# Attention stage of a decoder layer: sums through a three-bank ring, compact inverses, five transfers per chain, values of two blocks a visit

## The chip, the cores and the metric

One NeuronCore of a Trainium2 chip runs the whole program. The metric is the device time of one execution in microseconds (us). TensorE is written PE, VectorE DVE, ScalarE ACT, GpSimd POOL and the queue that issues most transfers SP.

## The reference

The program is one decoder layer on x of shape (2, 2048, 512): attention with 16 heads of 32, then a cross attention to 77 context rows, then a quantised feed-forward part. The change is in the attention alone, which computes for every batch and head

```
short = softmax(q ks^T / sqrt(32) - |i - j| (1 - decay)) vs
long  = softmax(q kl^T / sqrt(32)) vl
out   = sigmoid(mix) * short + (1 - sigmoid(mix)) * long
```

with 2048 queries and 2048 keys. All other stages are the same in both kernels.

## The kernel before

The attention works in units of one head and one kind of attention: w = 0 and 2 are "short", w = 1 and 3 "long", of two heads; four units make a pass, 16 passes make 64 units. The first and the last pass are written out, the others stand in a loop.

A unit has 16 key blocks of 128 keys (kb, also called a step i) and four query chunks of 512 (qt), so 64 chunks. For each unit five things happen, on different engines:

- **Maxima.** PE makes scores with queries on the partitions (`scores_for_max`, tile `scores_qk`, four PSUM banks used as two pairs). DVE reduces each pair of banks, 128x1024, to a row maximum (`max_pair`, L868). `negate` (L872), `turn_max` (L882) and SP's `place_max` (L735, four small transfers for a long unit, eight for a short one) put the negated maxima as one more row into the query operand.
- **Scores for exp.** PE makes the scores again with keys on the partitions (`scores_for_exp`, tile `scores_kq`, two PSUM banks), the maximum already subtracted. ACT takes exp of each 128x512 chunk into one of eight block buffers (`probs`, L852). Short units add small "kink" matmuls on the diagonal, in both kinds of scores.
- **Values.** `times_v` (L1025): four f32 matmuls, in four column groups of 32, shown as eight records, add a block's product to the bank `po`.
- **Sums.** The 16 blocks of a unit are added up elementwise, before PE's ones-matmuls (`count`, L1032) add over the partitions into the bank `pc`. POOL adds ten blocks (nine `tensor_tensor` of 128x2048, L804). Six blocks (0, 3, 6, 9, 12, 15) are summed by a chain of transfers of 1 MB that POOL issues: the first copies (L813), the others accumulate (L816), each after the one before has landed.
- **End of a unit.** DVE copies `po` out (`take`, L895, at i = 15), inverts `pc` in four pieces of 128x128 (`invert`, L900, at i = 7 to 10 of the next unit), multiplies (`weigh`, L910, i = 11) and, for the second unit of a head, adds the two (`mix`, i = 12). SP stores the result (L742) and loads the operands of the next pass.

PE's order is written by hand: in step i first the values of block i, then eight score chunks in the order exp, max, exp, max, max, exp, max, exp. ACT may write a block buffer only when the values, and the add or the landing of the transfer, of the block eight before are done. Every engine works through its list in order, and so does each queue.

Of the kernel before, what the change touches and what calls it, by code (L numbers as in the profile page):

```python
# [593 lines left out]

TURN_MAX = 10
SQUARE = 32
INVERT = 7
WEIGH = 11
MIX = 12


BY_DMA = (0, 3, 6, 9, 12, 15)
BY_POOL = tuple(b for b in range(KB) if b not in BY_DMA)
ADDS = len(BY_POOL) - 1
POURS = len(BY_DMA)
COUNT_ADDED = KB + 4
COUNT_POURED = KB + 6
POOL_ORDER = (0, 2, 4, 3, 5, 7, 6, 8, 10, 9, 11, 13, 12, 14, 15)
# [16 lines left out]

def attend(nc, qk_scr, v_scr, gates, kinkA, kinkB, pos_scr, attn_scr):

    with ExitStack() as ctx:
# [15 lines left out]

        oT = sb("o_T", [P, 2, BANK], F32)
        o_w = sb("o_weighed", [P, BANK], F32)
# [26 lines left out]
        counted = Rises(sem("a_counted"), UNITS, credit=1)  # L676
        counted_poured = Rises(sem("a_counted_poured"), UNITS, credit=1)
        taken = Rises(sem("a_o_taken"), UNITS, credit=1)
        inverted = Rises(sem("a_inverted"), UNITS * NQ)
# [27 lines left out]
        def _(sp):  # L707
# [21 lines left out]
            def place_max(w, n):  # L729

                sp.wait_ge(turned.sem, turned.at(n, w + 1))
                for dst in (q_op[w], q_up[w]) if w % 2 == 0 else (q_op[w],):
                    row = dst[MROW:MROW + 1, :].rearrange("o (t b c) -> o t b c", t=KB, c=SQUARE)
                    for b in range(P // SQUARE):
                        sp.dma_start(row[:, :, b, :], maxT[b * SQUARE:b * SQUARE + KB, w % 2, :]).then_inc(maxrow[w].sem, 16)  # L735

            def store(p, n):

                sp.wait_ge(mixed.sem, mixed.at(n, p + 1))
# [32 lines left out]
            one_pass(PASSES - 1, False, True)  # L772
            store(1, PASSES - 1)
# [4 lines left out]
        def _(pool):  # L778
            give_credit(pool, [maxed, expd, summed, added, counted, taken, weighed, counted_poured] + stored)
# [14 lines left out]
            def add(w, n, b):  # L794
# [3 lines left out]
                if b == BY_POOL[1]:  # L798
                    first = probs[:, BY_POOL[0], :]
                    wait_apart(pool, counted, counted.at(n, w - 1), passed)  # L800
# [3 lines left out]
                nc.gpsimd.tensor_tensor(total, first, probs[:, b % PBUF, :], ALU.add).then_inc(added.sem, 1)  # L804

            def pour(w, n, b):
# [4 lines left out]
                if i == 0:  # L811
                    wait_apart(pool, counted_poured, counted_poured.at(n, w - 1), passed)
                    nc.gpsimd.dma_start(total, probs[:, b % PBUF, :]).then_inc(landed.sem, 16)  # L813
                else:
                    wait_apart(pool, landed, landed.at(n, w // 2 * POURS + i), passed)
                    nc.gpsimd.dma_start(total, probs[:, b % PBUF, :], accum_op=ALU.add).then_inc(landed.sem, 16)  # L816
# [18 lines left out]
        def _(act):  # L835
            load_positions(act, 0)

            def one_pass(n, first, last):
                for w in range(UNITS):
                    for kb in range(KB):  # L840

                        u, b = divmod(w * KB + kb - PBUF, KB)
                        act.wait_ge(summed.sem, summed.at(n, u * KB + b + 1))
                        if b in BY_POOL:
                            act.wait_ge(added.sem, added.at(n, u * ADDS + adds_until(b)))
                        elif u >= 0 or not first:
                            landed = poured[u % 2]
                            act.wait_ge(landed.sem, landed.at(n, u // 2 * POURS + BY_DMA.index(b) + 1))
                        for qt in range(NQ):
                            k = (w * KB + kb) * NQ + qt  # L850
                            act.wait_ge(scoredB.sem, scoredB.at(n, k + 1))
                            nc.scalar.activation(probs[:, kb % PBUF, qt * BANK:(qt + 1) * BANK], pb[:, k % 2, :], ACT.Exp)\  # L852
                                .then_inc(expd.sem, 1)
# [5 lines left out]
            one_pass(PASSES - 1, False, True)  # L859

        @block.vector
        def _(dve):
# [29 lines left out]
            def take(w, n):  # L892

                dve.wait_ge(summed.sem, summed.at(n, (w + 1) * KB))
                nc.vector.tensor_copy(oT[:, w % 2, :], po[:, :]).then_inc(taken.sem, 1)  # L895

            def invert(w, n, r):

                dve.wait_ge(counted_poured.sem, counted_poured.at(n, w + 1))
                nc.vector.reciprocal(pc[:, r * P:(r + 1) * P], pc[:, r * P:(r + 1) * P]).then_inc(inverted.sem, 1)  # L900

            def weigh(w, n):

                dve.wait_ge(taken.sem, taken.at(n, w + 1))
                dve.wait_ge(inverted.sem, inverted.at(n, (w + 1) * NQ))
                if w == 2:
                    dve.wait_ge(mixed.sem, mixed.at(n, 1))
                elif w == 0 and (not isinstance(n, int) or n > 0):
                    dve.wait_ge(mixed.sem, mixed.before(n, 2))
                nc.vector.scalar_tensor_tensor(pc[:, :] if w % 2 else o_w[:, :], oT[:, w % 2, :],  # L910
# [787 lines left out]
```

## Time and profile before

| | before |
|---|---|
| median of 3 runs | 4902.25 us (4900.92 to 4911.55) |
| profiled execution: time / span | 4901.64 us / 4899.8 us |
| mean granted TensorE clock | 0.98 |
| PE / DVE / ACT / POOL busy over the span | 95% / 80% / 60% / 67% |
| attention, first to last copy of a unit's output | 598.8 to 3780.1 us |

A row of the timeline gives the start and the duration in us, the engine, the line, the operation, the tiles and shapes and, in brackets, how long the engine sat idle before it and for whom. "x4" is four instructions in a row. A PE matmul's duration (0.38 us for 512 columns) is longer than the distance from its start to the next one's (0.22 us), because they overlap.

### The profile page before, as it was taken

How to read it: one execution, taken by the hardware profiler on the slowest of the kernel's cores; microseconds unless marked ns; L12 is line 12 of the kernel's file. 1: busy time of each engine (PE TensorE's matmuls, PEld its weight loads, DVE VectorE, ACT ScalarE, POOL GpSimd, SP SyncE). 2: the span in 40 equal slices, each digit the busy share in tenths (PEclk: the TensorE clock that was granted, in tenths of full speed). 3: DMA queues.
4: the chain of work that ended last, by engine and by line, in shares of the span. 5: the costliest groups of instructions: out<-in, count | busy, mean ns of one | idle time of the engine just before them, and what ended most of it. 6: DMA issues, size and time to landing. Idle time of an engine off the chain costs nothing. (4 is left out here: it accounts for less than half of the span.)

```text
span 4899.8 us, 94453 instructions
## 1 busy us (share of the span) xinstructions
PE 4676.8 (95%) x30732; PEld 2051.3 (42%) x30732; DVE 3911.0 (80%) x4625; ACT 2928.4 (60%) x5106; POOL 3278.3 (67%) x1268
## 2 busy tenths in 40 slices
PE   8998999999999999999999999999998799999998
PEld 3444233333333333333333333333332577777776
DVE  7567888888888888888888888888884588888887
ACT  3222367676766766766666666766666355555554
POOL 0000399998989989888898989989897233333332
PEclk9999799999999999999999999999999799999999
DMA  5444366666676666666666676666765100000000
GB/s 171 126 140 129 84 154 154 152 151 160 146 156 151 157 157 146 159 144 157 153 146 159 144 158 155 157 154 146 165 135 118 59 27 27 20 27 27 27 23 12
DMA packets 216646, 592.18 MB, mean 121 GB/s; under 512 B 46259, under 2 KB 120115, under 8 KB 167157
## 3 DMA queue, kind: packets, MB, share of 16 engines
q0 software_dynamic: 55008, 400.58, 37.6%
q1 hardware_dynamic: 161135, 185.60, 12.8%
q8 instruction: 258, 4.23, 0.3%
q14 instruction: 207, 1.70, 0.1%
q10 hardware_dynamic: 38, 0.08, 0.0%
HBM read 123.56 MB, written 61.64 MB: 38 GB/s over the span
## 5 line engine op out<-in xcount | busy, mean ns | idle before, releaser
L852 ACT ACTIVATE probs_T<-scores_kq 128x512 f32<-128x512 f32 x4096 | 2247.2, 595 | 992.3 <-PE scores_kq L959 819.4
L868 DVE TENSOR_REDUCE rowmax_parts<-scores_qk 128x1 f32<-128x1024 f32 x2048 | 2398.3, 1210 | 546.1 <-PE scores_qk L959 541.9
L804 POOL TENSOR_TENSOR probs_added<-probs_added,probs_T 128x2048 f32<-128x2048 f32 x510 | 2386.1, 4679 | 48.8 <-POOL probs_added L804 37.5
L959 PE MATMUL scores_kq<-q_operand,k_operand 103*128 103x512 f16 (+3 forms) x3712 | 1277.7, 350 | 77.9 <-ACT probs_T L852 69.0
L959 PE MATMUL scores_qk<-k_operand,q_operand 96*128 96x512 f16 (+4 forms) x3712 | 1125.0, 351 | 32.7 <-DVE rowmax_parts L868 17.0
L1025 PE MATMUL outputs_T<-probs_T,v_operand 128*32 128x512 f32 x8192 | 1095.7, 607 | 1.0 <-ACT probs_T L852 1.0
L959 PEld LDWEIGHTS scores_kq<-q_operand,k_operand 103*128 103x128 f16 x3712 | 358.5, 97 | 1072.6 <-ACT probs_T L852 842.0
L959 PEld LDWEIGHTS scores_qk<-k_operand,q_operand 96*128 96x128 f16 (+1 forms) x3712 | 362.4, 98 | 336.8 <-DVE rowmax_parts L868 101.7
L1647 PE MATMUL f_gate_up<-w_gate_up,xq_T 128*128 128x256 f16 (+1 forms) x4608 | 494.3, 266 | 7.7 <-DVE hidden L1538 6.5
L1647 PEld LDWEIGHTS f_gate_up<-w_gate_up,xq_T 128*128 128x128 f16 x4608 | 421.1, 98 | 77.0 <-issue 24.3
L816 POOL DMA_DIRECT2D probs_poured<-probs_T x318 | 275.8, 867 | 255.7 <-DMA probs_poured<-probs_T 186.9
L959 PE MATMUL scores_kq<-q_operand_above,k_operand 103*128 103x512 f16 (+3 forms) x1152 | 400.5, 348 | 1.9 <-ACT probs_T L852 1.5
L959 PE MATMUL scores_qk<-k_operand,q_operand_above 102*128 102x512 f16 (+3 forms) x1152 | 368.8, 351 | 0.0
L1355 POOL TENSOR_TENSOR hidden_parts<-hidden_q,hidden_parts 128x768 f16<-128x768 f32 x64 | 97.9, 1529 | 349.9 <-ACT hidden_parts L1430 349.9
L780 POOL MEMSET ones<- 128x32 f32 x1 | 0.1, 124 | 464.0 <-POOLq L216 464.0
L804 POOL TENSOR_TENSOR probs_added<-probs_T 128x2048 f32<-128x2048 f32 x64 | 296.9, 4639 | 14.6 <-ACT probs_T L852 14.6
L959 PEld LDWEIGHTS scores_kq<-q_operand_above,k_operand 103*128 103x128 f16 x1152 | 110.0, 96 | 434.0 <-ACT probs_T L852 424.8
L1025 PEld LDWEIGHTS outputs_T<-probs_T,v_operand 128*32 128x32 f32 x8192 | 161.8, 108 | 261.8 <-issue 251.7
L900 DVE RECIPROCAL sums<-sums 128x128 f32<-128x128 f32 x256 | 243.8, 954 | 25.7 <-PE sums L1032 25.7
L555 PE MATMUL products_p<-xn_T_parts,w_qkv_parts 128*128 128x512 f16 x1152 | 254.5, 381 | 2.9 <-DVE xn_T_parts L408 1.5
L1632 PE MATMUL f_down<-w_down,hidden_T 128*128 128x512 f16 x1056 | 245.3, 382 | 0.0
L555 PEld LDWEIGHTS products_p<-xn_T_parts,w_qkv_parts 128*128 128x128 f16 x1152 | 112.9, 98 | 136.5 <-issue 4.1
(166 smaller groups left out, 4113.9 us busy)
## 6 DMA issues: line engine op xcount, KB each, us to landing
probs_poured<-probs_T POOLq DMA_DIRECT2D x382, 1024.0 KB, 7.6
qk_parts_dram<-qk_parts SPq DMA_DIRECT2D x96, 256.0 KB, 2.9
q_operand<-qk_parts_dram SPq DMA_DIRECT2D x192, 128.0 KB, 3.4
k_operand<-qk_parts_dram SPq DMA_DIRECT2D x192, 128.0 KB, 4.0
v_dram<-v_heads SPq DMA_DIRECT2D x16, 1024.0 KB, 6.4
v_operand<-v_dram SPq DMA_DIRECT2D x64, 256.0 KB, 6.5
q_operand_above<-qk_parts_dram SPq DMA_DIRECT2D x96, 128.0 KB, 2.8
x_groups<-x SPq DMA_DIRECT2D x8, 1024.0 KB, 9.4
```

Of the source, the lines that this page charges most:

```text
L555: last = nc.tensor.matmul(mm[:, m % 4, :], w_parts[:, a, c, m * P:(m + 1) * P], xT[:, u, c, b, :], start=c == 0 and a == b, stop=c == KT - ...
L780: nc.gpsimd.memset(ones[:, :], 1.0).then_inc(consts, 1)
L804: nc.gpsimd.tensor_tensor(total, first, probs[:, b % PBUF, :], ALU.add).then_inc(added.sem, 1)
L816: nc.gpsimd.dma_start(total, probs[:, b % PBUF, :], accum_op=ALU.add).then_inc(landed.sem, 16)
L852: nc.scalar.activation(probs[:, kb % PBUF, qt * BANK:(qt + 1) * BANK], pb[:, k % 2, :], ACT.Exp)\
L868: nc.vector.reduce_max(rowmax[:, w % 2, g // 2, g % 2:g % 2 + 1], half, AX.X).then_inc(maxed.sem, 1)
L900: nc.vector.reciprocal(pc[:, r * P:(r + 1) * P], pc[:, r * P:(r + 1) * P]).then_inc(inverted.sem, 1)
L959: return nc.tensor.matmul(out, lhsT, rhs, start=start, stop=stop, skip_group_check=True)
L1025: last = nc.tensor.matmul(po[qt * HD:(qt + 1) * HD, :], v_op[:, w, kb, :], probs[:, kb % PBUF, qt * BANK:(qt + 1) * BANK], start=kb == 0, ...
L1355: nc.gpsimd.tensor_tensor(h16[:, 1, a:a + w], hq[:, a:a + w], h16[:, 0, a:a + w], ALU.subtract)\
L1632: last = nc.tensor.matmul(pd[:, :], hT[:, c, a, :], wd[:, c, b, :], start=opens and c == first and a == b, stop=ends and c == first + coun ...
L1647: last = nc.tensor.matmul(pg[:, k % 2, g, 0:w], xqT[:, n % 2, c, a, :], w_up[:, c, g, b, at:at + w], start=c == 0 and a == b, stop=c == KT ...
```

## The change

- **Ring of three banks.** `scores_kq` has three banks. A unit has 66 ring slots: 64 chunks and two slots (`COUNT_SLOTS`, 27 and 36) into which the two ones-matmul groups of the unit before go. The bank `pc` is gone.
- **Values of two blocks a visit.** PE does `times_v` for steps i and i+1 together, then 16 score chunks in the order exp, max, max, exp, four times. Scores for exp run three chunks ahead of the values (`LEAD`).
- **Sums.** ACT writes exp of block 0 straight into `poured_sum`, so the chain has five transfers, all accumulating. POOL adds blocks 1, 2, 4, 5, 7, 8, 10, 11, 13, 14, still nine adds; the order of adds and transfers is changed (`POOL_ORDER`).
- **End of a unit.** ACT copies `po` (`take`) and the two sum banks (`copy_sums`). The sums are packed by two transfers to 128x16 (`pack_sums`), added (`merge`) and inverted (`invert`) by DVE at i = 9, stored to DRAM (`store_inverse`) and spread from there over 128x512 (`spread_inverse`). `weigh` is at i = 13, `mix` at i = 14, both on SBUF tiles. SP's list has the packing and storing ahead of `place_max`, the spreading behind it.

```diff
-INVERT = 7
-WEIGH = 11
-MIX = 12
-BY_DMA = (0, 3, 6, 9, 12, 15)
-POOL_ORDER = (0, 2, 4, 3, 5, 7, 6, 8, 10, 9, 11, 13, 12, 14, 15)
+INVERT = 9
+WEIGH = 13
+MIX = 14
+VISIT = 2
+LEAD = 3
+COUNTS_AT = (4, 6)
+BY_DMA = (3, 6, 9, 12, 15)
+BY_POOL = (1, 2, 4, 5, 7, 8, 10, 11, 13, 14)
+POOL_ORDER = (2, 3, 4, 5, 6, 7, 8, 9, 10, 11, 12, 13, 14, 15)
+def emitted(i):
+    return (i + VISIT) * NQ + LEAD
+COUNT_SLOTS = (emitted(COUNTS_AT[0]), emitted(COUNTS_AT[1]) + 1)
+RING = CHUNKS + 2
+BANKS = 3
...
-        pb = ps("scores_kq", [P, 2, BANK], F32)
+        pb = ps("scores_kq", [P, BANKS, BANK], F32)
-        pc = ps("sums", [P, BANK], F32)
+        def block_of(w, kb):
+            return poured_sum[:, w % 2, :] if kb == 0 else probs[:, kb % PBUF, :]
...
@@ block.sync @@
+            def pack_sums(w, n, j):
+                wait_apart(sp, sums_out, sums_out.at(n, 2 * w + j + 1), passed)
+                wait_apart(sp, merged, merged.at(n, w), passed)
+                sp.dma_start(sums_c[:, j, :], sums[::HD, j, :]).then_inc(packed[j].sem, 16)
+            def store_inverse(w, n):
+                wait_apart(sp, inverted, inverted.at(n, w + 1), passed)
+                wait_apart(sp, inv_spread, inv_spread.at(n, w - 1), passed)
+                sp.dma_start(inv_scr[w % 2:w % 2 + 1, :].rearrange("o (p i) -> (o p) i", i=COMPACT), inv_c[:, :])\
+                    .then_inc(inv_stored.sem, 16)
+            def spread_inverse(w, n):
+                wait_apart(sp, inv_stored, inv_stored.at(n, w + 1), passed)
+                wait_apart(sp, weighed, weighed.at(n, w - 1), passed)
+                rows4 = inv_scr[w % 2].rearrange("(q n) -> q n", q=NQ).unsqueeze(1).to_broadcast([NQ, HD, BANK])
+                sp.dma_start(inv[:, w % 2, :], rows4).then_inc(inv_spread.sem, 16)
...
                 for w in range(UNITS):
+                    back = unit_before(w, n, first)
+                    if back:
+                        for j in range(2):
+                            pack_sums(*back, j)
+                        store_inverse(*back)
                     if after(w, n, last):
                         place_max(*after(w, n, last))
+                    if back:
+                        spread_inverse(*back)
...
@@ block.scalar @@
+            def copy_sums(w, n, j):
+                act.wait_ge(counted[j].sem, counted[j].at(n, w + 1))
+                act.wait_ge(packed[j].sem, packed[j].at(n, w))
+                nc.scalar.copy(sums[:, j, :], pb[:, COUNT_SLOTS[j] % BANKS, :]).then_inc(sums_out.sem, 1)
+            def take(w, n):
+                act.wait_ge(summed.sem, summed.at(n, (w + 1) * KB))
...
+                nc.scalar.copy(oT[:, w % 2, :], po[:, :]).then_inc(taken.sem, 1)
...
@@ block.vector @@
-                nc.vector.reciprocal(pc[:, r * P:(r + 1) * P], pc[:, r * P:(r + 1) * P]).then_inc(inverted.sem, 1)
+            def merge(w, n):
...
+                nc.vector.tensor_tensor(sums_c[:, 0, :], sums_c[:, 0, :], sums_c[:, 1, :], ALU.add).then_inc(merged.sem, 1)
+            def invert(w, n):
+                dve.wait_ge(inv_stored.sem, inv_stored.at(n, w))
+                nc.vector.reciprocal(inv_c[:, :], sums_c[:, 0, :]).then_inc(inverted.sem, 1)
             def weigh(w, n):
                 dve.wait_ge(taken.sem, taken.at(n, w + 1))
+                dve.wait_ge(inv_spread.sem, inv_spread.at(n, w + 1))
...
@@ block.tensor @@
+            def bank_free(w, n, r):
+                r -= BANKS
...
-                        times_v(w, n, i)
-                        counts(w, n, i)
...
+                    for i in range(0, KB, VISIT):
+                        for step in range(i, i + VISIT):
+                            times_v(w, n, step)
+                        if back and i == COUNTS_AT[0]:
+                            count_added(*back)
+                        if back and i == COUNTS_AT[1]:
+                            count_poured(*back)
+                        at = emitted(i)
+                        for step in range(i, i + VISIT):
+                            for half in range(2):
+                                scores(at)
+                                maxima(step, 2 * half)
+                                scores(at + 1)
+                                at += 2
```

## Rows read from the trace of the kernel before

**Rows 1.** Busy time by engine in the attention; columns PE, PEld, DVE, ACT, POOL
```profile
598.83:3780.12 3181.29, 3094.67 (x20017) 1028.41 (x20019) 2613.55 (x2508) 2210.55 (x4030) 2872.35 (x944) 1.00 0.67 152
```

**Rows 2.** The copy of a unit's output: all 64, duration and first and last start
```profile
L895 DVE COPY o_T<-outputs_T x64: 678/680/692, 598.8 to 3780.1; 128x512 f32<-128x512 f32 x64
```

**Rows 3.** Waits from 600 to 3700 us: total, times, longest
```profile
POOL probs_poured L816 <- DMA probs_poured<-probs_T: 183.1, 60, 5.4
ACT probs_T L852 <- DMA probs_poured<-probs_T: 110.8, 77, 3.4
```

**Rows 4.** Timeline of POOL around the end of one unit
```profile
2513.63 0.87 POOL L816 DMA_DIRECT2D probs_poured<-probs_T  x1
...
2523.73 0.87 POOL L816 DMA_DIRECT2D probs_poured<-probs_T  x1
2524.34 4.83 POOL L804 TENSOR_TENSOR probs_added<-probs_added,probs_T 128x2048 f32<-128x2048 f32 x1
2534.18 0.87 POOL L816 DMA_DIRECT2D probs_poured<-probs_T  x1 [5.01 <-DMA probs_poured<-probs_T]
2534.97 0.64 POOL L813 DMA_DIRECT2D probs_poured<-probs_T  x1
```

**Rows 5.** Timeline of ACT, its waits for transfers: the one at the same place
```profile
2533.71 3.37 ACT L852 ACTIVATE probs_T<-scores_kq 128x512 f32<-128x512 f32 x6 [2.57 <-DMA probs_poured<-probs_T]
```

**Rows 6.** Timeline of DVE: the shortest full unit, by the copies of its output
```profile
2111.80 0.68 DVE L895 COPY o_T<-outputs_T 128x512 f32<-128x512 f32 x1
...
2160.56 0.68 DVE L895 COPY o_T<-outputs_T 128x512 f32<-128x512 f32 x1
```

**Rows 7.** Timeline of one undisturbed step, all engines
```profile
2476.45 0.39 PE L959 MATMUL scores_kq<-q_operand,k_operand 103*128 103x512 f16 x1
...
2476.87 2.29 ACT L852 ACTIVATE probs_T<-scores_kq 128x512 f32<-128x512 f32 x4 [0.67 <-PE scores_kq L959]
...
2477.11 0.59 PE L959 MATMUL scores_qk<-k_operand,q_operand 96*128 96x512 f16 x2
...
2477.53 2.35 DVE L868 TENSOR_REDUCE rowmax_parts<-scores_qk 128x1 f32<-128x1024 f32 x2 [0.61 <-PE scores_qk L959]
...
2478.09 0.38 PE L959 MATMUL scores_kq<-q_operand,k_operand 103*128 103x512 f16 x1
...
2478.41 1.06 PE L1025 MATMUL outputs_T<-probs_T,v_operand 128*32 128x512 f32 x8
...
2479.40 0.39 PE L959 MATMUL scores_kq<-q_operand,k_operand 103*128 103x512 f16 x1
```

**Rows 8.** Timeline: values and a count back to back, then the next score
```profile
2485.06 1.07 PE L1025 MATMUL outputs_T<-probs_T,v_operand 128*32 128x512 f32 x8
...
2486.91 0.39 PE L959 MATMUL scores_kq<-q_operand,k_operand 103*128 103x512 f16 x1
```

**Rows 9.** Groups of DVE from 600 to 3700 us: busy us, mean ns
```profile
L900 DVE RECIPROCAL sums<-sums 128x128 f32<-128x128 f32 x244 | 233.2, 956 | 0.0
...
L882 DVE STREAM_TRANSPOSE negmax_T<-negmax 128x32 f16<-128x32 f16 x61 | 11.9, 195 | 0.0
```

**Rows 10.** Timeline of SP: the eight transfers of the maxima of a short unit
```profile
2559.80 2.55 SPq L735 DMA_DIRECT2D q_operand<-negmax_T  x4
2562.39 2.98 SPq L735 DMA_DIRECT2D q_operand_above<-negmax_T  x4
```

**Rows 11.** Transfers of the whole span: KB each, median us from issue to landing
```profile
probs_poured<-probs_T POOLq DMA_DIRECT2D x382, 1024.0 KB, 7.6
...
q_operand<-qk_parts_dram SPq DMA_DIRECT2D x192, 128.0 KB, 3.4
...
v_operand<-v_dram SPq DMA_DIRECT2D x64, 256.0 KB, 6.5
...
attn_T<-attention_dram SPq DMA_DIRECT2D x32, 256.0 KB, 2.8
...
q_operand<-negmax_T SPq DMA_DIRECT2D x256, 1.0 KB, 2.1
```

More of the change, by code:

```diff
@@ L838, in one_pass @@
             def one_pass(n, first, last):
                 for w in range(UNITS):
+                    back = unit_before(w, n, first)
                     for kb in range(KB):
[L842 to L848, printed above, removed]
@@ L849, in one_pass @@
-                        for qt in range(NQ):
[L850 to L853, printed above, removed]
+                        block_free(w, n, kb, first)
+                        for qt in range(NQ):
+                            c = kb * NQ + qt
+                            for j in range(2):
+                                if back and ring_of(c) == COUNT_SLOTS[j] + 1:
+                                    copy_sums(*back, j)
+                            act.wait_ge(scoredB.sem, scoredB.at(n, w * CHUNKS + c + 1))
+                            nc.scalar.activation(block_of(w, kb)[:, qt * BANK:(qt + 1) * BANK], pb[:, ring_of(c) % BANKS, :],
+                                                 ACT.Exp).then_inc(expd.sem, 1)
+                            if back and c == LEAD - 1:
+                                take(*back)
@@ L923, in one_pass @@
                     for i in range(KB):
-                        if i == KB - 1:
-                            take(w, n)
-                        if back and INVERT <= i < INVERT + NQ:
-                            invert(*back, i - INVERT)
+                        distance, chunks = chunks_of(i)
+                        unit = after(w, n, last, distance)
+                        if back and i == INVERT:
+                            merge(*back)
                         if back and i == WEIGH:
                             weigh(*back)
-                        distance, chunks = chunks_of(i)
-                        unit = after(w, n, last, distance)
+                        if back and i == MIX and back[0] % 2:
+                            mix(back[0] // 2, back[1])
                         for c in chunks[::2] if unit else ():
@@ L935, in one_pass @@
                                 negate(*unit)
-                            if i == TURN_MAX and c == chunks[0]:
-                                turn_max(*ahead)
+                            if c == chunks[0]:
+                                if back and i == INVERT:
+                                    dve.wait_ge(merged.sem, merged.at(back[1], back[0] + 1))
+                                    invert(*back)
+                                if i == TURN_MAX:
+                                    turn_max(*ahead)
+                        if back and i == INVERT and not unit:
+                            dve.wait_ge(merged.sem, merged.at(back[1], back[0] + 1))
+                            invert(*back)
                         if i == TURN_MAX and ahead and not unit:
                             turn_max(*ahead)
-                        if back and i == MIX and back[0] % 2:
-                            mix(back[0] // 2, back[1])
             one_pass(0, True, False)
@@ L947, in _ @@
             one_pass(PASSES - 1, False, True)
[L948 to L949 removed]
+            dve.wait_ge(packed[0].sem, packed[0].at(PASSES - 1, UNITS))
+            invert(UNITS - 1, PASSES - 1)
             weigh(UNITS - 1, PASSES - 1)
```

168 lines of the change are left out of this document (87 added, 81 removed).

## The prediction, made before the change was run

> **What bounds the kernel now.** I read the windows first, because they say which engines can be the bound. In the attention PE is busy 3094.7 of 3181.3 us and POOL 2872.4, or 97% and 90%; DVE has 82% and ACT 69% [rows 1]. The 64 copies of a unit's output start from 598.8 to 3780.1 us, so 63 units take 50.50 us each [rows 2]. Of a busy PE one must ask whether it could be faster; of POOL, whether it ever waits for more work.
>
> The waits answer the second question. POOL waits for its own transfers 183 us in 60 times, about once a unit, and ACT, which feeds everything, waits 111 us for the same transfers [rows 3]. The timeline shows where. A transfer and two adds take 2523.73 - 2513.63 = 10.10 us. Between transfers 12 and 15 there is one add only, so 15 has to wait until 12 has landed, and is issued at 2534.18, 10.45 us after 12 [rows 4]. At the same moment (2533.71) ACT gets on, after 2.57 us: its step 4 writes the buffer of block 12 [rows 5]. So POOL's list in a unit is 4 x 10.10 + 0.61 + 4.83 (transfer 12, add 14) + 0.79 (transfer 15) = 46.6 us, plus some 3 us (183.1 over 61 units) and smaller waits: near the 50.5. POOL with its chain sets most units.
>
> PE stands close behind: the shortest full unit is 2160.56 - 2111.80 = 48.76 us [rows 6]. Its step: eight score matmuls from 2476.45 to 2478.41, 1.96 us; two kinks of a quarter's length (0.11) and the gap ahead of the values (2478.09 to 2478.41 is one matmul and 0.10) taken off, 0.217 each. The values take until 2479.40, 0.99 us [rows 7]; a second group of eight directly behind adds 2486.91 - 2485.06 - 0.99 = 0.86 [rows 8]. Sixteen steps of 1.74 + 0.10 + 0.99 are 45.3, two counts 1.7, kinks on average 1.3 (short units alone have them), together 48.3; the other 0.4 lies in the steps with an inversion, 0.96 us more of DVE [rows 9].
>
> **The change, part by part.**
>
> *Chain and order of POOL.* Transfer 0 goes, and every pair of transfers now has two adds between. POOL's list: 4 x 10.10 + 0.61 + 4.83 = 45.8 us, with no wait, as 10.10 is more than the median landing of 7.6 [rows 11]; only a landing like that of [rows 4] would cost 0.3. POOL is then 4 us under the unit and stops being the bound. Gain: down to what PE needs. That ACT writes block 0 elsewhere costs nothing; its new waits lie a unit back.
>
> *Values of two blocks a visit.* The gaps around the values (0.10, and 0.99 - 0.86 = 0.13) come 8 times instead of 16: -1.9 us a unit for PE alone. But the 16 score chunks of a visit now come in one piece, with four pairs for DVE, and there are two pairs of banks. From the first score (0): the pair is scored at 0.22 and 0.43; DVE starts 0.42 after the second (2477.11 to 2477.53 [rows 7]), at 0.85; two reductions take 2.35 [rows 7], the second ends at 3.20; only then may the fourth pair be scored, from 3.27 (0.07 to get there), then the last score at 3.71; values from 4.03, for 1.85; next visit at 5.88. PE alone would need 5.42. In the kernel before, the two pairs of a step are spread evenly and two steps take 5.66. Eight visits: 47.0; two counts 1.7; kinks outside the two reductions 0.5; `turn_max` (0.2, [rows 9]) inside them 0.2; `mix`, every other unit, 0.1: **49.5 us** a unit.
>
> *Three banks.* The walk shows what they are for: exp, 0.54 a chunk, gets through three chunks while PE does values; with the 0.42 ahead of exp ([rows 7] again) the seventh score waits for the fourth exp until 2.76, where it stands anyway. Two banks would not do. Gain here zero, its absence would cost.
>
> *Work moved from DVE to ACT.* DVE loses four inversions of 0.96 [rows 9] and the copy of 0.68 [rows 2], 4.5 us; it gets two operations on 128x16 (below 0.2 each, as the transpose). That ends the 0.4 us of the inversion steps, which the sum of 49.5 has no more. ACT gets three copies of some 0.6: in the walk they push exp by 0.3, within the slack ahead of the fourth pair. Cover gone, 0.9 us a unit.
>
> *The row of maxima.* Scores for exp run ahead, so the first chunk of the next unit is wanted in visit 12 instead of in step 14. `turn_max` is done 2.2 us into the scores of visit 10, the eight transfers take 5.6 us to issue [rows 10] and the last lands 2.1 after its issue [rows 11]: 9.3. It is wanted at 5.88 + 0.2 + 2.6 = 8.7. Some 0.6 late, which moves the end of that visit by 0.4 in short units ahead, none where four transfers do: **+0.2** a unit.
>
> *Inverse over DRAM.* Behind these eight stands `spread_inverse` in SP's list. It is issued at 7.8. Its landing is not in the trace: 256 KB took 2.8 us when little else ran and 6.5 at the end of a list of loads; 128 KB took 3.4 [rows 11]. I take 3.0, nearer to the low row, since it stands alone in its queue. It lands at 10.8; DVE comes to `weigh` at 6.08 + 3.2 = 9.3 and waits, with all maxima behind it. After `weigh` (0.7) and two reductions the first one of visit 14 starts about 13.9 instead of 13.2: 0.7 in half of the units, **+0.35**. Where the next unit is long, the same comes 2.8 us earlier and costs nothing. The Trainium skill (DMA: Bandwidth & Descriptors, Anatomy of one DMA) gives 2.0 us plus the bytes at 436 GB/s; an estimate by that page is 2.6 us for this transfer, and the forecast would be some 13 us lower. For the 1 MB transfers of this trace it would give 4.4 against a median of 7.6 [rows 11], so it is too short where they run.
>
> Packing and storing have 8 us and are over before. Loads of SP start 3 us later (`mix` at i = 14) and are wanted more than a unit later. *The end:* behind the last unit a copy, three transfers (2.1, 2.1 and 2.8 or more, each with its issue) take the place of 3.4 us of inversions: +5 us once; PE and all else wait there.
>
> *Sum:* 49.5 + 0.2 + 0.35 = 50.05 us a unit, 0.45 less than 50.50; 63 units give -28, the end +5. Against the profiled execution's 4901.6, which is 0.6 below the median of the runs: **4878 us**.
>
> **The rivals.**
> - *No lateness:* maxima and inverse come in time (an issue below 0.6 and a landing of 2.5 do it). 49.5 a unit: 4844.
> - *The inverse late, slower than before:* from a landing of about 3.9 us on, the wait at `weigh` eats the whole gain; at 5 us it costs 1.35 a unit, 51.05 in all: 4941; at 6.5, 51.8: near 4990. For it: the share of DMA time in this stage is 0.67 [rows 1]. Against: one transfer, alone in its queue.
> - *The transfers still set the pace* (the change does not do what it says): if 12 and the others land after more than 10 us because SP's loads and four new transfers get in their way, the unit stays at 50.5: 4907. For it [rows 4]; against it 7.6 [rows 11] and one transfer of 1 MB fewer a unit.
> - *DVE's round trip does not bind:* if the pairs were free early, PE's own 5.42 would leave 43.4 + 1.7 + 1.3 + small waits, some 47 a unit: 4686. Against it speak the two pairs of banks.
>
> **How the numbers follow.** Forecast 0.40, no lateness 0.20, late inverse 0.20, transfers still binding 0.14, no round trip 0.06. A measurement of this kernel tells 0.2%, about 10 us, from no change, so the bounds are 4892 and 4912. The forecast's own range, 4855 to 4905, lies for three quarters below 4892: faster 0.30 + 0.20 + 0.06 and 0.03 of the transfers' case, 0.59. Same: 0.08 of the forecast, 0.07 of the transfers, 0.02 of the late inverse, 0.17. Slower: 0.24. The range 4810 to 4950 leaves out the no-round-trip case and the worst half of the late inverse.
>
> **What would show it.** POOL's waits for transfers gone, and ACT's. Visits of 5.9 us, with PE waiting for the row maxima ahead of the third and fourth pair of each; if they are 5.5, the walk is wrong. DVE waiting for a transfer at `weigh` when the next unit is short, PE for the maxima's transfer there. Exp of four chunks during the values of PE. A chain of POOL still longer than 49 us, or DVE waits of more than 2 us at `weigh`, would make the forecast wrong.

## The result and the profile after

The changed kernel takes 5400.8 us (median of 4 runs, 5390.88 to 5406.15) against 4901.59 us for the kernel before beside it: a ratio of 1.1011, 95% interval [1.0988, 1.1034]. It is 10% slower. 4878 us were forecast and 4950 was the upper end of the range. The profiled execution took 5404.6 us, its span is 5402.8 us.

All of it lies in the attention. ACT's copies of a unit's output, which took over from those of [rows 2], start from 593.35 to 4284.05 us: 58.58 us a unit instead of 50.50, and over 63 units that is 509 us, a little more than the 503 us by which the span grew. Busy time by engine in this stage (columns as in [rows 1]), changed kernel:

```profile
592.00:4284.00 3692.00, 3276.44 (x20035) 1124.82 (x20031) 2587.84 (x2320) 2225.89 (x4219) 2825.96 (x881) 0.94 0.56 118
```

Read beside [rows 1] it splits the loss in two. PE sits idle for 3692.0 - 3276.4 = 415.6 us, before for 86.6: 329 us more. And PE is busy 182 us longer with the same matmuls (20,035 records against 20,017), at a granted clock of 0.94 instead of 1.00. No engine became the bound: the shares of PE, DVE, ACT and POOL all fell. So this is a loss by waiting, and the waits say for whom (700 to 4200 us; total, times, longest):

```profile
POOL probs_added L864 <- ACT probs_T L936: 794.1, 131, 15.6
ACT probs_T L936 <- PE scores_kq L1050: 782.7, 603, 5.8
...
PEld scores_qk L1050 <- DVE rowmax_parts L958: 547.4, 929, 5.2
DVE o_T L997 <- DMA sums_inverse<-sums_inverse_dram: 345.8, 60, 8.8
...
PE scores_qk L1050 <- DVE rowmax_parts L958: 209.0, 199, 4.9
...
PE scores_kq L1050 <- DMA q_operand_above<-negmax_T: 70.7, 24, 4.1
...
PE scores_kq L1050 <- DMA q_operand<-negmax_T: 56.9, 30, 3.0
```

POOL's and ACT's waits for the 1 MB transfers [rows 3] are gone, as forecast. POOL waits for ACT instead, ACT for PE, PE for DVE and for the row of maxima, and DVE for the inverse. The chain ends at DVE and at transfers. What DVE does there shows in the views of the tiles `o_T` and `sums_compact` of the changed kernel (shortest, median, longest ns, then first and last start):

```profile
L997 DVE SCALAR_TENSOR_TENSOR o_T<-o_T,gates,sums_inverse x64: 750/752/3534, 649.4 to 4299.0; 128x512 f32<-128x512 f32 x64
L1004 DVE TENSOR_TENSOR o_mixed<-o_T x32: 678/680/4866, 707.8 to 4299.8; 128x512 f32<-128x512 f32 x32
```

```profile
L986 DVE TENSOR_TENSOR sums_compact<-sums_compact x63: 939/3420/3760, 627.8 to 4269.6; 128x16 f32<-128x16 f32 x63
```

`merge`, one addition of 128x16, takes 3.4 us in the median, some fifteen times the inversion of the same size (0.235). The timeline of the changed kernel at one of them, with what follows:

```profile
2505.47 4.82 POOL L864 TENSOR_TENSOR probs_added<-probs_added,probs_T 128x2048 f32<-128x2048 f32 x1
...
2506.58 3.75 DVE L986 TENSOR_TENSOR sums_compact<-sums_compact 128x16 f32<-128x16 f32 x1
...
2507.53 1.92 PE L1127 MATMUL outputs_T<-probs_T,v_operand 128*32 128x512 f32 x16
...
2511.51 0.60 PE L1050 MATMUL scores_qk<-k_operand,q_operand 96*128 96x512 f16 x2 [1.74 <-DVE rowmax_parts L958]
...
2512.75 1.04 PE L1050 MATMUL scores_qk<-k_operand,q_operand 96*128 96x512 f16 x2 [0.20 <-DVE rowmax_parts L958]
```

The merge ends at 2510.33, POOL's addition at 2510.29. In all 63 units the merge ends 0.04 us after the addition that was running when it started. DVE doesn't compute for 3.4 us; it is held until GpSimd is done. PE then stands for 1.74 us, and from 2512.75 its records are longer: 1.04 instead of 0.60 for two matmuls, and the values that follow (second row below) take 2.84 instead of the 1.92 above. The granted clock is 0.51 from 2512.7 to 2519.6 us and was 1.00 from 2500 to 2509: the lower of the chip's two levels (1.2 GHz) instead of the higher (2.4 GHz), about 1 us after PE's pause. The rest of the same unit, with SP's queue:

```profile
2514.27 2.88 SPq L764 DMA_DIRECT2D q_operand<-negmax_T  x4
2517.19 4.53 SPq L764 DMA_DIRECT2D q_operand_above<-negmax_T  x4
2522.01 0.60 SPq L784 DMA_DIRECT2D sums_inverse<-sums_inverse_dram  x1
```

```profile
2517.56 2.84 PE L1127 MATMUL outputs_T<-probs_T,v_operand 128*32 128x512 f32 x16
2528.76 0.75 DVE L997 SCALAR_TENSOR_TENSOR o_T<-o_T,gates,sums_inverse 128x512 f32<-128x512 f32 x1 [5.21 <-DMA sums_inverse<-sums_inverse_dram]
2530.70 0.61 PE L1050 MATMUL scores_qk<-k_operand,q_operand 96*128 96x512 f16 x1 [4.08 <-DVE rowmax_parts L958]
```

The transfer that spreads the inverse is issued at 2522.01, and `weigh` gets on at 2528.76, 6.75 us later. DVE idles for 5.21 us with every reduction behind it, and PE for 4.08. `weigh` waited like this in all 64 units, 382 us in all; from the issue of the transfer to the start of `weigh` it was 4.9 to 9.2 us, 7.5 in the median.

Why did the same kind of work not hold DVE before? The `weigh` and `mix` of the kernel before start during POOL's additions too (61 of 64 and 27 of 32), and none of them is held. Timeline of the kernel before:

```profile
2405.91 4.53 POOL L804 TENSOR_TENSOR probs_added<-probs_added,probs_T 128x2048 f32<-128x2048 f32 x1 [0.18 <-POOL probs_added L804]
...
2406.32 0.74 DVE L910 SCALAR_TENSOR_TENSOR sums<-o_T,gates,sums 128x512 f32<-128x512 f32 x1
...
2410.99 4.83 POOL L804 TENSOR_TENSOR probs_added<-probs_added,probs_T 128x2048 f32<-128x2048 f32 x1
...
2411.98 0.68 DVE L918 TENSOR_TENSOR o_mixed<-o_weighed,sums 128x512 f32<-128x512 f32 x1
```

Both are over after 0.74 and 0.68 us, with the addition running on. There one of the two tensor inputs, `pc` (shown as `sums`), lies in PSUM. The change gave that bank to the ring and put both inputs of `merge`, `weigh` and `mix` into SBUF. The Trainium skill (SBUF — State Buffer, Who interferes with whom) says that a DVE instruction with two SBUF inputs and a GpSimd instruction that reads SBUF shut each other out for a whole instruction, that the order of issue decides who waits, and that a reduction never does. The 63 merges agree with it, and so do the 0.74 and 0.68 us with one input in PSUM; the prediction had not weighed it.

### The profile page after: what moved, and what is told of

It reads as the page before. It is cut to its first block and busy times, and to the rows that moved or that the text cites. A ratio compares the mean times of both kernels' runs of the same rounds, so it can differ in the third digit from the quotient of the medians.

```text
span 5402.8 us, 95671 instructions
## 1 busy us (share of the span) xinstructions
PE 4841.2 (90%) x30732; PEld 2145.3 (40%) x30732; DVE 3879.8 (72%) x4432; ACT 2943.6 (54%) x5297; POOL 3230.8 (60%) x1204
## 5 line engine op out<-in xcount | busy, mean ns | idle before, releaser
L936 ACT ACTIVATE probs_T<-scores_kq 128x512 f32<-128x512 f32 x3840 | 2031.4, 608 | 871.9 <-PE scores_kq L1050 835.3
L1050 PE MATMUL scores_kq<-q_operand,k_operand 103*128 103x512 f16 (+3 forms) x3712 | 1172.5, 365 | 175.0 <-DMA q_operand_above<-negmax_T 78.4
L1050 PE MATMUL scores_qk<-k_operand,q_operand 96*128 96x512 f16 (+4 forms) x3712 | 1037.0, 365 | 258.4 <-DVE rowmax_parts L958 221.0
L1127 PE MATMUL outputs_T<-probs_T,v_operand 128*32 128x512 f32 x7680 | 981.6, 628 | 0.1
L1050 PEld LDWEIGHTS scores_qk<-k_operand,q_operand 96*128 96x128 f16 (+1 forms) x3712 | 295.0, 100 | 712.4 <-DVE rowmax_parts L958 534.7
L1127 PEld LDWEIGHTS outputs_T<-probs_T,v_operand 128*32 128x32 f32 x7680 | 211.4, 113 | 517.8 <-issue 266.5
L1050 PE MATMUL scores_kq<-q_operand_above,k_operand 103*128 103x512 f16 (+3 forms) x1152 | 341.0, 354 | 0.9 <-ACT probs_T L936 0.5
L997 DVE SCALAR_TENSOR_TENSOR o_T<-o_T,gates,sums_inverse 128x512 f32<-128x512 f32 x64 | 50.9, 795 | 382.1 <-DMA sums_inverse<-sums_inverse_dram 382.1
L986 DVE TENSOR_TENSOR sums_compact<-sums_compact 128x16 f32<-128x16 f32 x63 | 212.5, 3374 | 30.5 <-DMA sums_compact<-sums 30.5
L936 ACT ACTIVATE probs_poured<-scores_kq 128x512 f32<-128x512 f32 x256 | 142.3, 599 | 151.2 <-PE scores_kq L1050 150.5
```

Source lines behind the costliest of these rows:

```text
L936: nc.scalar.activation(block_of(w, kb)[:, qt * BANK:(qt + 1) * BANK], pb[:, ring_of(c) % BANKS, :], ACT.Exp).then_inc(expd.sem, 1)
L986: nc.vector.tensor_tensor(sums_c[:, 0, :], sums_c[:, 0, :], sums_c[:, 1, :], ALU.add).then_inc(merged.sem, 1)
L997: nc.vector.scalar_tensor_tensor(oT[:, w % 2, :], oT[:, w % 2, :], gates[:, 3 + w % 2:4 + w % 2], inv[:, w % 2, :], ALU.mult, ALU.mult).th ...
L1050: return nc.tensor.matmul(out, lhsT, rhs, start=start, stop=stop, skip_group_check=True)
L1127: last = nc.tensor.matmul(po[qt * HD:(qt + 1) * HD, :], v_op[:, w, kb, :], block_of(w, kb)[:, qt * BANK:(qt + 1) * BANK], start=kb == 0, s ...
```

## The experiments

There are three suspects: the hold (DVE held by POOL's additions), the wait (for the inverse from DRAM) and the visits of two blocks. The kernel before took 4900 to 4905 us beside the runs. Each ratio is to the kernel before.

**e1, the merge with one input.** A reduction over both halves of one tile does the same addition:

```diff
-nc.vector.tensor_tensor(sums_c[:, 0, :], sums_c[:, 0, :], sums_c[:, 1, :], ALU.add)
+nc.vector.tensor_reduce(sums_m[:, :], sums_c.rearrange("p j c -> p c j"), AX.X, ALU.add)
```

> The changed kernel with one edit: merge is a tensor_reduce over one strided input into a tile of its own, in place of the tensor_tensor with two inputs in SBUF. Theory A (merge is held until GpSimd's running add ends, because both read SBUF through a shared port): merge falls from 3.37 us to about 0.25 us, 3.1 us a unit, and as 1.2 us of DVE's slack covered part of it, the program gains 120 to 250 us, to 5150 to 5280. Rival B (merge is slow in itself, or the inverse's late landing hides whatever merge gives back): merge gets short but the wait at weigh grows by as much, program within 30 us of 5401.

5364.8 us, ratio 1.0945 [1.0923, 1.0967]: near what rival B gave, not the 120 to 250 us of theory A. The merge is at 0.18 us, so the hold was real; but only 36 us come back. The groups of DVE in e1 (busy, mean ns, idle before):

```profile
L998 DVE SCALAR_TENSOR_TENSOR o_T<-o_T,gates,sums_inverse 128x512 f32<-128x512 f32 x64 | 64.3, 1004 | 496.8 <-DMA sums_inverse<-sums_inverse_dram 496.8
...
L987 DVE TENSOR_REDUCE sums_merged<-sums_compact 128x16 f32<-128x32 f32 x63 | 11.2, 177 | 30.5 <-DMA sums_compact<-sums 30.5
```

DVE reaches `weigh` sooner and waits there longer, 497 us in all against 382 in the changed kernel. The two delays stand in one row; with one taken out the next is waited for in its place.

**e2, no wait for the inverse.** `weigh` multiplies by a constant 1 and waits for no transfer. The division by the sums is left out; all transfers are still made.

```diff
-dve.wait_ge(inv_spread.sem, inv_spread.at(n, w + 1))
-... inv[:, w % 2, :], ALU.mult, ALU.mult)
+... inv[:, 1, :], ALU.mult, ALU.mult)
```

> The changed kernel, but weigh multiplies by a constant 1 tile and does not wait for the inverse from DRAM; the division by the softmax sums is left out, all transfers stay. The profile shows 363 us of DVE waits there. Theory A: that wait is the larger part of the loss: 5050 to 5200. But weigh and mix, with two inputs in SBUF, then meet GpSimd's adds (in the changed kernel all 64 ran while GpSimd had nothing to do) and some of them take up to 4.8 us in place of 0.75. Rival B (the two-block visit itself costs the 10%): above 5330.

5263.1 us, ratio 1.0737 [1.0716, 1.0759], between the ranges of theory A and rival B. 138 us come back, and the time that `weigh` waited it now spends held:

```profile
L998 DVE SCALAR_TENSOR_TENSOR o_T<-o_T,gates,sums_inverse 128x512 f32<-128x512 f32 x64 | 264.8, 4138 | 0.0
L988 DVE TENSOR_TENSOR sums_compact<-sums_compact 128x16 f32<-128x16 f32 x63 | 214.7, 3408 | 28.6 <-DMA sums_compact<-sums 28.6
```

In the changed kernel `weigh` took 0.75 us: 63 of the 64 started while no addition of POOL was running, because by the time the inverse had come POOL had run out of work. Here 62 of the 64 start during an addition. The wait hid the hold.

**e3, visits of one block.**

```diff
-VISIT = 2
+VISIT = 1
```

> The changed kernel with VISIT = 1: values of one block a visit, all else as it is. Theory A (the end of a unit is what costs): the same stalls at merge and weigh remain, 5300 to 5420. Rival B (two blocks a visit, DVE's round trip and the lower clock cost the time): close to 4950.

5445.2 us, ratio 1.1109 [1.1087, 1.1131]: slower than the changed kernel, and above both ranges. With the other two causes in place, going back to visits of one block gains nothing; `weigh` and `mix` were held more (means of 1.89 and 2.80 us), the merge less (1.93).

**e4, the chain of five alone.** The kernel before, with five accumulating transfers, block 0 written straight into their sum, and the changed order of POOL. Banks, visits and the end of a unit stay as before.

```diff
-BY_DMA = (0, 3, 6, 9, 12, 15)
-POOL_ORDER = (0, 2, 4, 3, 5, 7, 6, 8, 10, 9, 11, 13, 12, 14, 15)
+BY_DMA = (3, 6, 9, 12, 15)
+POOL_ORDER = (2, 3, 4, 5, 6, 7, 8, 9, 10, 11, 12, 13, 14, 15)
...
+            return poured_sum[:, w % 2, :] if kb == 0 else probs[:, kb % PBUF, :]
```

> The kernel before with one part of the change alone: exp of block 0 goes straight to the transfers' sum, five transfers in the chain, two adds between each two, the new order of GpSimd. Theory A (GpSimd's chain set most units before): its waits for transfers go, the unit falls from 50.5 to 48.8 to 49.2, the program to 4790 to 4830. Rival B (the waits move to PE or elsewhere, or the transfers land just as late): within 15 us of 4902.

4820.4 us (4818.69 to 4824.43), ratio 0.9836 [0.982, 0.9852]: faster than both kernels, 82 us under the one before, as theory A said. Busy time in its attention (columns as in [rows 1]):

```profile
600.00:3600.00 3000.00, 2988.01 (x19457) 1002.08 (x19449) 2570.14 (x2465) 2138.41 (x3894) 2732.18 (x852) 1.00 0.64 135
```

PE is busy 99.6% of it, and POOL waits no more for its transfers. A unit takes 49.28 us. This part of the change is a gain, so with it in place the other parts lose some 580 us.

**e5, no holds at all.** The changed kernel with `merge`, `weigh` and `mix` as reductions with one input, and no wait for the inverse. The gate's product and the division are left out; every transfer is still made.

```diff
-nc.vector.scalar_tensor_tensor(oT[:, w % 2, :], oT[:, w % 2, :], gates[...], inv[:, w % 2, :], ALU.mult, ALU.mult)
+nc.vector.tensor_reduce(oT[:, w % 2, :], oT[:, w % 2, :].unsqueeze(2), AX.X, ALU.max)
...
-nc.vector.tensor_tensor(o_mix[:, p, :], oT[:, 0, :], oT[:, 1, :], ALU.add)
+nc.vector.tensor_reduce(o_mix[:, p, :], oT.rearrange("p j q -> p q j"), AX.X, ALU.add)
```

> The changed kernel with the merge, weigh and mix each a tensor_reduce that reads SBUF through one input, and with no wait of weigh for the inverse from DRAM; the division by the sums and the weight of the gate are left out, all transfers stay. What is left is the walk of the visits (5.9 us), the counts, the maxima's row and the clock. Theory A (the walk was right, the loss is the holds by GpSimd and the wait at weigh): a unit of 49.5 to 50.5 us, 4850 to 4930, granted clock back at 0.99 in the attention. Rival B (the two-block visit with three banks costs more than its walk): above 5000.

5077.4 us, ratio 1.0357 [1.0337, 1.0378]: the hold and the wait together are worth 323 us. Yet the kernel is slower than before, in the range of rival B, so a third loss is left. Units with a long one ahead take 50.7 us, those with a short one ahead 56. Timeline of POOL, SP and PE in e5:

```profile
2455.39 0.87 POOL L878 DMA_DIRECT2D probs_poured<-probs_T  x1
```

```profile
2454.96 3.22 SPq L765 DMA_DIRECT2D q_operand_above<-negmax_T  x4
```

```profile
2464.16 0.28 PE L1051 MATMUL scores_kq<-q_operand,k_operand 103*128 103x128 f16 x1 [5.29 <-DMA q_operand_above<-negmax_T]
...
2466.62 2.77 PE L1128 MATMUL outputs_T<-probs_T,v_operand 128*32 128x512 f32 x16
```

PE stands 5.29 us for the eighth transfer of the row of maxima, and comes back at the lower clock. The trace has the landings too: POOL's 1 MB transfer, issued at 2455.39, lands at 2463.76, the eighth small one, issued at 2456.86, at 2464.04. In 29 of the 30 such units after 700 us the eighth lands within 0.6 us behind POOL's transfer (0.3 in the median).

**e6, the inverse brought back first.** e1, with `spread_inverse` ahead of `place_max` in SP's list; the whole computation.

```diff
+                        spread_inverse(*back)
                     if after(w, n, last):
                         place_max(*after(w, n, last))
-                    if back:
-                        spread_inverse(*back)
```

> The changed kernel with the one-input merge and spread_inverse directly behind store_inverse in SP's list, ahead of the maxima's transfers. Theory A: the inverse is issued some 6 to 8 us earlier in short units and lands before weigh needs it, so DVE's wait for the transfer nearly goes, but weigh then meets GpSimd's adds and is held for 3 to 4 us, as in the run without the wait: 5180 to 5260. Rival B (the transfer itself is what is slow, wherever it is issued): DVE waits more than 3 us a unit still, above 5300.

5304.2 us, ratio 1.082 [1.0799, 1.0842]. The wait went as theory A said (`weigh` waits 64 us in all), but the time is above its range, as `weigh` and `mix` are held:

```profile
L997 DVE SCALAR_TENSOR_TENSOR o_T<-o_T,gates,sums_inverse 128x512 f32<-128x512 f32 x64 | 153.1, 2392 | 64.0 <-DMA sums_inverse<-sums_inverse_dram 63.9
L1004 DVE TENSOR_TENSOR o_mixed<-o_T 128x512 f32<-128x512 f32 x32 | 62.2, 1945 | 0.1
```

PE's wait for the row of maxima rose to 201 us (`q_operand_above`) and 75 us (`q_operand`). A better place in the queue for one transfer made the next ones in it late.

**e7, e5 with visits of one block.** `VISIT = 1` in e5, and the same left out.

> As the run without holds (merge, weigh and mix on one input, no wait for the inverse, division and gate left out), with VISIT = 1. Theory A (DVE's round trip lengthens the two-block visit from 5.66 to 5.9 us, and the holds hid it): a unit of 48.3 to 49 us, 4770 to 4830, below the two-block one by 50 to 100 us. Rival C (one block a visit is slower in this layout for a reason of its own, as it was with the holds by 44 us): above the two-block run.

4768.5 us, ratio 0.9727 [0.9708, 0.9747]. So, with the hold and the wait out, the visits of two blocks cost 309 us, where the 50 to 100 of theory A had been expected. A unit takes 48.42 us, and after the first units PE waits for no row of maxima. Windows of the attention, e7 first, then e5:

```profile
596.91:3647.22 3050.31, 3042.80 (x20017) 1062.55 (x20019) 2422.42 (x2319) 2263.42 (x4219) 2826.59 (x881) 1.00 0.68 143
```

```profile
594.70:3951.60 3356.90, 3134.73 (x20023) 1094.01 (x20026) 2386.54 (x2320) 2203.21 (x4218) 2827.49 (x881) 0.97 0.62 130
```

Of the 307 us between them 215 are idle time of PE, 153 of these the wait for the row of maxima, and 92 the same matmuls at a lower clock.

**e8, the hold alone.** e4, and once a unit (i = 5) one addition of 128x16 whose result nobody reads.

```diff
+                        if i == 5:
+                            nc.vector.tensor_tensor(probe[:, 2, :], probe[:, 0, :], probe[:, 1, :], ALU.add)
```

> The kernel before with the five-transfer chain (the run of 4820) and one more DVE instruction a unit: a tensor_tensor of 128x16 with both inputs in SBUF, at i = 5, whose result nobody reads. Theory A (held by GpSimd's running add): its duration is anything from 0.1 to 4.8 us, 2 to 3 on average, and ends 0.04 us after an add ends; DVE has some 0.5 us a step to spare, so the program loses 60 to 160 us, to 4880 to 4980. Rival (small instructions are just cheap): about 0.1 us each, no change.

4938.4 us, ratio 1.0076 [1.0059, 1.0093], 118 us above e4 and in the range of theory A. In e8:

```profile
2411.02 4.53 POOL L810 TENSOR_TENSOR probs_added<-probs_added,probs_T 128x2048 f32<-128x2048 f32 x1 [0.18 <-ACT probs_T L864]
...
2411.66 3.92 DVE L941 TENSOR_TENSOR probe<-probe 128x16 f32<-128x16 f32 x1
```

Its end is 2415.58, that of the addition 2415.55. The 64 probes take 3.91 us in the mean, and each ends 0.03 to 0.04 us after an addition.

**e9, e5 without the transfer of the inverse.** `spread_inverse` goes too; e5's omissions stay.

> The kernel of e5_no_holds (visits of two blocks; merge, weigh and mix as reductions with one input; the multiplication by the inverse, the gate's product and the wait for the inverse left out) with the transfer that brings the inverse back left out too. Its time was 5077 us, with units of 50.7 and 56 us in turn; the short unit waited 5.1 us for the row of maxima, which landed 7.2 us after its issue. Theory A, the row is late because the 256 KB transfer of the inverse shares the DMA engines with it: the wait falls to 1 us or below, the clock of TensorE stays at its higher level, short units take 51 to 52 us, the time is 4900 to 4960 us. Theory B, the row is late by its own issue and landing, and by the loads of the next unit: the wait stays at 4 us or more, the time is 5050 to 5090 us.

5068.8 us, ratio 1.0344 [1.0323, 1.0365]. Theory B holds: PE's wait for the row is what it was, 153 us in 30 times. The 256 KB of the inverse are not why the row is late.

**e10, the changed kernel mended as far as it goes.** The whole computation: e6 with `VISIT = 1` and `mix` as a reduction. `weigh` alone keeps two SBUF inputs.

> The changed kernel with its whole computation, in visits of one block, with the merge and the mix as reductions with one input from SBUF and the inverse brought back ahead of the row of maxima. Only weigh keeps two inputs from SBUF. Theory A, what costs is the holding of VectorE by GpSimd's additions and the late inverse: e7_no_holds_visit1 took 4768 us, and weigh held for up to 3 us a unit adds up to 190 us, if half of it reaches TensorE some 95: 4850 to 4960 us. Theory B, the round trip of sums and inverse has a further cost that the reductions of e7 took away with the wait: above 5000 us.

5166.2 us, ratio 1.0545 [1.0528, 1.0563], above what theory A gave and in the range of theory B. A unit takes (4035.1 - 596.8) / 63 = 54.58 us, 6.2 more than in e7. Groups of DVE in e10 from 700 to 3900 us:

```profile
L997 DVE SCALAR_TENSOR_TENSOR o_T<-o_T,gates,sums_inverse 128x512 f32<-128x512 f32 x59 | 220.4, 3735 | 133.8 <-DMA sums_inverse<-sums_inverse_dram 133.8
```

`weigh` waits 2.3 us and takes 3.7, 3.1 more than the reduction in its place in e7. The expectation had counted half of the hold and nothing for the wait. Together they are some 5.3 us a unit, and the unit grew by 6.2: all of it reached TensorE, and more.

**e11, e8's control.** The same probe as a reduction with one SBUF input.

```diff
-nc.vector.tensor_tensor(probe[:, 2, :], probe[:, 0, :], probe[:, 1, :], ALU.add)
+nc.vector.tensor_reduce(probe[:, 2, :], probe[:, 0:2, :].rearrange("p j c -> p c j"), AX.X, ALU.add)
```

> The control of e8_port_probe: the kernel of e4_chain5_alone with one added VectorE instruction a unit at the same place and of the same size (128x16, result unread), as a reduction with one input from SBUF. Theory A, the 4 us of the probe in e8 come from its two SBUF inputs beside GpSimd's addition: this one takes about 0.2 us, and the time is that of e4, 4820 to 4830 us. Theory B, any added VectorE instruction at that place is held or costs: its mean is above 1 us, the time above 4880 us.

4820.2 us, ratio 0.9837 [0.9821, 0.9854]: the time of e4. Row of the probe in e11, and behind it that of e8 (shortest, median, longest ns):

```profile
L941 DVE TENSOR_REDUCE probe<-probe x64: 176/177/179, 568.6 to 3656.7; 128x16 f32<-128x32 f32 x64
```

```profile
L941 DVE TENSOR_TENSOR probe<-probe x64: 360/3965/4239, 569.5 to 3775.5; 128x16 f32<-128x16 f32 x64
```

Same place, same size, same bytes, 0.18 against 3.97 us. The two differ in the operation too, but an addition as such is not held: `mix` of the kernel before, a `tensor_tensor` with one input in PSUM, takes 0.68 us amid POOL's additions. The second SBUF input is the cause.

**e12, e10 with the wait but without the hold.** `weigh` becomes a reduction that still waits for the inverse; the products with the gate and the inverse are left out.

> The kernel of e10_mended_visit1 (5166 us, units of 54.6 us) with weigh as a reduction with one input from SBUF that still waits for the inverse; its multiplication by the gate and by the inverse is left out, so the output is not the attention's. In e10 weigh waited 2.3 us a unit for the inverse and then took 3.7 us, where e7_no_holds_visit1 (4768 us, units of 48.4 us) had neither. Theory A, the hold by GpSimd's addition and the wait each cost TensorE their own length: without the hold a unit falls by 3 us or somewhat more, to 51 to 52 us, and the time to 4940 to 5000 us. Theory B, the wait alone starts the rest (a late row of maxima, GpSimd behind ACT, the lower clock), and the hold is hidden behind it: less than 60 us are gained, the time stays above 5100 us. Theory C, one stall more or less is caught up within the unit and only their sum is too long: below 4850 us.

4904.8 us (10 runs, 4886.25 to 4927.53), ratio 1.0 [0.9984, 1.0016], between theories A and C. It differs from e10 in `weigh` alone, so there the hold costs 261 us, or 4.1 us a unit for 3.0 us of hold: more than its own length. Against e7 it is 136 us (2.2 us a unit for 2.5 us of waiting); that is the price of the wait together with the place of `spread_inverse`, which in e7 stands behind `place_max`. Windows of the attention, e12 first, then e10:

```profile
596.50:3768.40 3171.90, 3091.31 (x20017) 1061.19 (x20019) 2421.49 (x2319) 2270.96 (x4219) 2821.54 (x881) 0.99 0.66 137
```

```profile
596.80:4035.10 3438.30, 3173.17 (x20017) 1088.28 (x20019) 2626.22 (x2319) 2270.27 (x4218) 2834.81 (x881) 0.95 0.62 127
```

Of the 266 us between them, 184 are idle time of PE and 82 the same matmuls at a lower clock (0.95 against 0.99). The lower clock is about the surplus.

## Why the prediction was wrong

Three terms of the sum failed: the small operations on DVE, the landing of the inverse and the row of maxima. They stand first here.

*Operations moved to DVE, "two operations on 128x16 (below 0.2 each, as the transpose)": the step that failed first.* The inversion did take 0.24 us. The merge took 3.4, because both its inputs lie in SBUF and POOL was adding. The prediction priced an instruction by its size and looked up a neighbour of that size which has one input; it never asked where the inputs lie, nor what POOL does meanwhile. The same holds for `weigh` and `mix`, which the prediction took at their old lengths (0.7 for `weigh`): those (0.74 and 0.68 us, amid additions) were of instructions with one input in PSUM. No rival had this mechanism. Shown by e1, e8 with e11, and e10 with e12.

*The landing of the inverse, 3.0 us: failed.* It was 6.75 us in the unit shown and 7.5 in the median. The case was there as a rival ("at 6.5, 51.8: near 4990", chance 0.20), and the upper row of [rows 11], 6.5, was the nearer one. "Alone in its queue" did not hold: in the unit shown the row of maxima is issued directly ahead of it and seven loads directly behind it, from 2522.80 on. POOL's 1 MB transfer is not what it met there (one lands at 2522.10, the next is issued at 2526.16). Which of its neighbours lengthens it is not separated. "Where the next unit is long" it was to cost nothing; there `weigh` waited 142 us in 32 times. And the merge, held, delays `turn_max` behind it on DVE, with that the eight transfers, and so the inverse behind these.

*The row of maxima, +0.2 us a unit: failed.* In the changed kernel PE waits for it 128 us in 54 times between 700 and 4200 us, some 2 us a unit; in e5 it is 5.1 us in each second one. The prediction put the row 0.6 us late. In e5 SP starts the eight at 2452.45 and PE gets on at 2464.16: 11.7 us instead of the 7.1 of the prediction (9.3 - 2.2). The difference is the landing of the last one: 6.9 us in the median where 2.1 were taken. There it is issued some 1.5 us behind a 1 MB transfer of POOL and lands with it; in e7 it is issued 8.6 us behind one (both medians) and lands after 1.7. The prediction had no term for where in POOL's cycle of 10 us the row is sent. e9 excludes the inverse's transfer, which stands behind the row. That POOL's transfer is the cause is read from these landings; no run moves it alone.

*Visits of two blocks, a DVE round trip of 5.88 us.* The length was right, its price was not. A visit of the changed kernel with no wait goes from 2503.45 to 2509.39, 5.94 us, and later ones take 5.89. What it does to the time had been seen as a loss of 0.2 against two steps of before; it is 309 us in e5 against e7, 153 of them the wait for the row of maxima and 92 the lower clock. The rest, some 60, is idle time of the walk itself: DVE's chain has no slack left, and each small operation is added to it. In e5 these are 0.18 + 0.24 + 0.19 + 0.20 + 0.68 + half of 1.23, 2.1 us a unit, where the sum counted 0.3 (`turn_max` and `mix`). It would account for the unit of 50.7 without a wait for the row, instead of 49.5; that is argued, not separated.

*Chain and order of POOL: POOL freed, gain down to what PE needs.* Right, and its effect undersized: e4 has it alone and gains 82 us, where all gains of the forecast came to 28.

*Three banks, and ACT's copies: no gain, no cost.* Not separated. e7 has both, with visits of one block, and is 52 us under e4 with a smaller computation.

*Clock.* The sum took every matmul at the clock of [rows 1]. PE was then busy 182 of the 511 us longer. It is no cause of its own, it follows PE's pauses: the mean clock of the attention was 1.00 in e4 and e7, where PE hardly stands, and 0.99, 0.95 and 0.94 in e12, e10 and the changed kernel, with 81, 265 and 416 us of idle time. In e8 PE idles for 127 us, but never for more than 1.5 us at a time, and the clock stays at 1.00.

The ladder, then, from 5401: the holds and the wait for the inverse out, 5077 (e5); visits of two blocks out, 4768 (e7). In visits of one block the two of the first step have prices of their own: 261 us for the hold of `weigh`, 136 for the wait. They don't add up simply, since each covers the next (e1, e2, e3, e6 gave back 36, 138, -44 and 97 us). So the change lost both by what it moved out of PSUM and by one thing that it set out to do, the visits of two blocks. Of the runs with the whole computation, the one with its first part alone (e4) is the fastest. The 4768 us of e7 leave out the gate and the division, and no run shows a way to add them there without a hold or a wait.

## What to carry to other kernels

Price an instruction by where its operands lie and what GpSimd does meanwhile, not by its size alone: beside a GpSimd that adds for 90% of the time, a VectorE instruction gets one SBUF input and the other from PSUM, or is written as a reduction. When several delays stand in a row on one engine, take all of them out at once to see the floor (e5, e7), then put them back one by one; taking one out alone tells only which comes next. Ask of each operand that a reordering wants earlier whether the transfer that brings it can be issued earlier as well, and which large transfer will be under way then.

## What the runs showed of the hardware

- A VectorE addition of 128x16 with two SBUF inputs, started during a GpSimd addition of 128x2048 (4.5 to 4.8 us), ends some 0.04 us after it: 3.4 us on average over 63 merges, 3.9 over 64 probes. A product of 128x512 held so ended 0.55 us after the addition (62 in e2). A reduction of the same bytes as the probe takes 0.18 us there, and a product of 128x512 with one input in PSUM 0.74.
- A transfer of 256 KB from DRAM, issued by SP right behind the row of maxima, was waited for until 4.9 to 9.2 us after its issue (median 7.5) at a DMA share of 0.56; the estimate in the prediction by the Trainium skill (DMA: Bandwidth & Descriptors, Anatomy of one DMA) was 2.6. That page's figure is for transfers that GpSimd issues; this one is SP's.
- Four 1 KB transfers to `q_operand_above` took 3.22 and 4.53 us to issue. The last of them landed in the median 6.9 us after its issue in e5, sent some 1.5 us behind a 1 MB transfer of POOL and landing 0.3 us behind it, and 1.7 us after its issue in e7, sent 8.6 us behind one.
- About 1 us after a pause of 1.74 us PE's matmuls followed each other at 0.43 us instead of 0.22, and the values took 2.84 us instead of 1.92, at a granted clock of 0.51. Over the attention, 265 us of idle time in e10, with waits of up to 4.7 us, went with a mean clock of 0.95, and 127 us in e8, with waits of up to 1.5 us, with 1.00.
